# Macaron block on one core: first expert FFN on two hidden buffers, row 0's transposes inside the routing, another order of loads, stores and row ends

## What is computed

```
x = x + 0.5 * ffn(layernorm(x));  x = x + attn(layernorm(x));  x = x + 0.5 * ffn(layernorm(x))

ffn:  probs = softmax(x0 @ switch_w.T + switch_b)   # x0: all 512*512 values of a row, 8 experts
      gate, idx = top_k(probs, 2)
      h = gelu(xh @ w1[idx] + b1[idx])              # 16 heads of 32 features, the same expert for a whole row
      o = sum over k of gate[k] * (h @ w2[idx] + b2[idx])
      return (x + o) @ w3.T + b3
attn: q, k, v, a, g = split(x @ w_in.T); q = q*rsqrt(mean(q*q)); k = tanh(k); a = clip(sigmoid(a+2), 0.6, 0.9995)
      memory = linear recurrence of k*v with decay a along the tokens, in chunks of 64 tokens
      y = sigmoid(g)*(q*memory) + (1-sigmoid(g))*v;  return y @ w_out.T
```

## Time and profile before

| | before |
|---|---|
| runs, median (lowest to highest) | 574.57 us (573.95 to 575.01), 3 runs |
| the profiled execution | 573.66 us, of which 571.9 us are the span of the trace |
| PE busy | 507.7 us, 89% of the span |
| DVE / ACT / POOL busy | 417.1 / 232.1 / 137.1 us |
| mean granted clock of PE | 0.967 of full speed |
| chain of waits that ended last | PE 65%, DVE 16%, "issue" 7%, SP's queue 3%, POOL 3%, DMA 3%, ACT 2% |

### The profile page before, as it was taken

How to read it: one execution, slowest core, us unless ns; L and a number is a source line. 1 busy time by engine, 2 the same in 40 slices (tenths; PEclk the granted TensorE clock), 3 DMA queues, 4 the chain that set the end, 5 groups by cost and what they waited for, 6 DMA issues and landing times.

```text
span 571.9 us, 9061 instructions
## 1 busy us (share of the span) xinstructions
PE 507.7 (89%) x3372; PEld 361.8 (63%) x3372; DVE 417.1 (73%) x778; ACT 232.1 (41%) x390; POOL 137.1 (24%) x145
## 2 busy tenths in 40 slices
PE   0557899999899999989999999999998747999997
PEld 0444676567586666758666666866666634677776
DVE  4869887997864777796467788656868568988752
ACT  0145544432814233281422337243342237656540
POOL 5140004254002224401322430133330100321220
PEclk9976999999999999999999999999999877899999
DMA  8994004000002000010200000035535620013112
GB/s 345 409 388 202 1 1 166 1 0 1 37 19 92 2 0 2 1 38 19 92 0 0 0 0 37 18 128 194 188 144 182 216 74 2 19 47 119 41 53 92
DMA packets 15797, 48.21 MB, mean 84 GB/s; under 512 B 1169, under 2 KB 1169, under 8 KB 14225
## 3 DMA queue, kind: packets, MB, share of 16 engines
q1 hardware_dynamic: 15760, 47.73, 22.3%
HBM read 39.34 MB, written 8.39 MB: 83 GB/s over the span
## 4 chain that ended last, share of the span: by engine, by line
PE 65%; DVE 16%; issue 7%; SPq 3%; POOL 3%; DMA 3%; ACT 2%; DVEq 0%; POOLq 0%; ACTq 0%
PE bank L727 9%; PE bank L408 9%; PE bank L732 9%; PE bank L728 9%; PE bank L410 8%; PE bank L409 8%; DMA route_w<-in_switch_w 3%; SPq L434 2%; POOL rs L1132 2%; DVE h_lo L1342 2%; PE bank L531 2%; DVE xt_lo L1353 1%; PE bank L580 1%; PE bank L562 1%; PE bank L638 1%
## 5 line engine op out<-in xcount | busy, mean ns | idle before, releaser
L727 PE MATMUL bank<-xh,win_hi 128*128 128x512 f32 x300 | 133.7, 446 | 0.0
L728 PE MATMUL bank<-xl,win_hi 128*128 128x512 f32 x300 | 118.1, 394 | 0.0
L732 PE MATMUL bank<-xbf,win_lo 128*128 128x512 bf16 x312 | 85.3, 382 | 0.0
L1132 POOL TENSOR_TENSOR rs<-ms,neg_half 128x16 f32<-128x16 f32 x16 | 49.8, 3114 | 137.8 <-ACT ms L950 137.8
L727 PEld LDWEIGHTS bank<-xh,win_hi 128*128 128x128 f32 x300 | 56.4, 188 | 21.0 <-issue 3.2
L728 PEld LDWEIGHTS bank<-xl,win_hi 128*128 128x128 f32 x300 | 56.5, 188 | 11.1
L1119 POOL TENSOR_TENSOR xa<-xa,tables 128x512 f32<-128x512 f32 x28 | 38.9, 1401 | 71.4 <-DVE z_lo L1360 39.0
L408 PE MATMUL bank<-w_hi,z_hi 128*128 128x512 f32 x128 | 51.6, 403 | 0.0
L410 PE MATMUL bank<-w_hi,z_lo 128*128 128x512 f32 x128 | 50.1, 391 | 0.0
L409 PE MATMUL bank<-w_lo,z_hi 128*128 128x512 f32 x128 | 50.1, 391 | 0.0
L732 PEld LDWEIGHTS bank<-xbf,win_lo 128*128 128x128 bf16 x312 | 25.5, 98 | 35.5 <-issue 21.3
(11 more groups left out here) (199 smaller groups left out, 1010.4 us busy)
## 6 DMA issues: line engine op xcount, KB each, us to landing
raw<-in_w_in SPq DMA_DIRECT2D x4, 1280.0 KB, 9.9
route_w<-in_switch_w SPq DMA_DIRECT2D x4, 1280.0 KB, 5.4
route_w<-in_switch_w SPq DMA_DIRECT2D x9, 512.0 KB, 15.5
xa<-in_x SPq DMA_DIRECT2D x4, 1024.0 KB, 5.6
route_w<-in_switch_w SPq DMA_DIRECT2D x2, 2048.0 KB, 15.3
out<-x SPq DMA_DIRECT2D x16, 256.0 KB, 2.0
x_dram<-x1p SPq DMA_DIRECT2D x12, 256.0 KB, 2.0
xa<-x_dram SPq DMA_DIRECT2D x3, 1024.0 KB, 5.7
```

The costliest lines, as they stand in the source:

```text
L727: pe.matmul(bank[:], win_hi[:, c, r, k, :], xh[:, k, :], start=(k == 0), stop=False)
L728: pe.matmul(bank[:], win_hi[:, c, r, k, :], xl[:, k, :], start=False, stop=False)
L732: mm = pe.matmul(bank[:], win_lo[:, c, r, k, :], xbf[:, k, :], start=False, stop=(k == KC - 1))
L1132: pool.tensor_tensor(rs[:], ms[:], neg_half[:], ALU.pow).then_inc(s_rs, 1)
```

## The change

- **FFN 0** uses both hidden buffers, and ACT casts the second expert's half (`second_hi`); DVE splits chunk 1 right after chunk 0 and forms `w3_lo` after `split_hidden(0, 3)`.
- **Tables** are loaded in two parts: b3 ahead of the last routing weights, the rest behind them.
- **Attention chunk on ACT:** `y_out(b, c-1)` stands ahead of `decay`. The Gelu table is loaded after the first `t1_out` of the row end.
- **Row 3 on DVE:** the statistics of routing chunk 3 move from the gap of attention chunk 3 to behind chunk 2.
- **Routing:** row 0's transposes `t1(B, 0..3)` stand between routing chunks 1 and 2; `xt_split(B, 0..3)` ahead of `choose(1)`. ACT loads the Exp table before them.
- **Order on SP:** the load of `xa` between `late_weights` 2 and 3; after the routing first `xa1`, then, once it has landed, the stores of row 3, then `x1p`.
- **f = 5's normed tokens** are written by ACT (`row_norm(B + 1, 1, xnw)`, after the Gelu table, before `gelu(B, 0)`) and no longer by DVE.
- **POOL's bias adds** for f = 4 run as soon as the `xt_split`s are done.

```diff
 def hid_set(f, c):
-    return hid1 if is_late(f) and c % 2 else hid0
+    return hid1 if hid_bufs(f) == 2 and c % 2 else hid0      # hid_bufs: 2 if is_late(f) or f == 0
 # SP
-sp.dma_start(tables[:], tables_in).then_inc(s_small, 16)
+sp.dma_start(b3_half, tables_in[:, 0:D]).then_inc(s_b3l, 16)
 weight_load(NT - 1)
+sp.dma_start(tables[:, D:TABLES], tables_in[:, D:TABLES]).then_inc(s_small, 16)
...
 late_weights(2)
+sp.wait_ge(s_rna, 1)
+sp.dma_start(xa[:], row_of(x2_dram, 0)).then_inc(s_xa, 16)
 late_weights(3)
 sp.wait_ge(s_y, KC * B)
 late_piece(60, 64)
-sp.wait_ge(s_rna, 1)
-sp.dma_start(xa[:], row_of(x2_dram, 0)).then_inc(s_xa, 16)
+sp.wait_ge(s_rm, 2 * NT)
+sp.dma_start(xa1[:], row_of(x2_dram, 1)).then_inc(s_xa1, 16)
+sp.wait_ge(s_xa1, 16)
+for t in range(NT):
+    store_x2(B - 1, t, x1, job_last(f"A{t}"))
 sp.wait_ge(s_rna, 2)
 sp.dma_start(x1p[:], row_of(x2_dram, 2)).then_inc(s_xa2, 16)
-for t in range(NT):
-    store_x2(B - 1, t, x1, job_last(f"A{t}"))
-sp.wait_ge(s_rm, 2 * NT)
-sp.dma_start(xa1[:], row_of(x2_dram, 1)).then_inc(s_xa1, 16)
 # PE, route(phase)
+if phase == 1 and t == 2:
+    for c in range(KC):
+        t1(B, c, B - 1, False)
...
-for c in range(KC):
-    t1(B, c, B - 1, False)
-    if c == 1:
-        logits(1)
+logits(1)
 # ACT
 def ffn(f, begun):
     t1_out(f, 0)
+    load_table(ACT.Gelu)               # was the end of begun(), after t1_out(f, 1)
     t1_out(f, 1)
...
 # group(b, c), behind ms
+if c >= 1:
+    y_out(b, c - 1)
 act.activation(decay[:], src, ACT.Sigmoid, bias=two[:]).then_inc(s_ina, 1)
 src = bank(JOB_V)
-if c >= 1:
-    act.wait_ge(s_y, KC * b + c)
-    y_out(b, c - 1)
...
 # first_ffn: second_hi(0, c) behind every gelu(0, c)
 # end of attention
 route_norm(NT - 1)
-first_row()
+row_norm(B, 0, xn_0)
+load_table(ACT.Exp)
 for c in range(KC):
     t1_out(B, c)
 route_exp(1)
 load_table(ACT.Gelu)
+row_norm(B + 1, 1, xnw)                # waits for s_rm 2*NT and for xa1
 # POOL
+pool.wait_ge(s_xtl, KC * (B + 1))
+for c in range(KC):
+    residual_bias(B, c)                # was: each after z_split(B, c)
 # DVE, FFN 0
 split_hidden(0, 0, None)
-ve.wait_ge(s_w3h, 1)
-ve.scalar_tensor_tensor(out=w3_lo[:], ...).then_inc(s_w3l, 1)
+split_hidden(0, 1, None)
 for c in range(KC):
-    if c < KC - 1:
-        split_hidden(0, c + 1, job)
+    if c < 2:
+        split_hidden(0, c + 2, job_first(f"O{c}"))
+    if c == 1:
+        ve.wait_ge(s_w3h, 1)
+        ve.scalar_tensor_tensor(out=w3_lo[:], ...).then_inc(s_w3l, 1)
     z_split(0, c, x_bank[c])
 # DVE, attention(B - 1): gap of chunks 0 to 2: route_var(FEW + c, route_stats(FEW + c))
 # behind chunk 0, 1: route_norm(FEW + c); behind chunk 2: route_var(FEW + 3, route_stats(FEW + 3))
 route_norm(LAST + NT - 1)
+for c in range(KC):
+    xt_split(B, c)
 choose(1)
-xt_split(B, 0)
 select(0, B, 0)
-for c in range(1, KC):
-    xt_split(B, c)
 by_half(1)
 select(0, B, 1, lambda: gate(1))
 hidden_lo(B, 0)
 hidden_lo(B, 1)
-normalise(B + 1, 1)
```

More of the change, by code:

```diff
@@ L251, in ffn_input, with is_first, hid_bufs @@
             return xa, s_xa, 16 * f
+        def is_first(f):
+            return isinstance(f, int) and f == 0
+        def hid_bufs(f):
+            return 2 if is_late(f) or is_first(f) else 1
         def hid_set(f, c):
-            return hid1 if is_late(f) and c % 2 else hid0
+            return hid1 if hid_bufs(f) == 2 and c % 2 else hid0
         banks = [ctx.enter_context(nc.psum_tensor(f"bank{i}", [P, 512], F32)) for i in range(8)]
@@ L869, in gelu @@
                     act.wait_ge(s_h, H_JOBS * f + TOPK * c + k + 1)
-                    if is_late(f) or not (isinstance(f, int) and f == 0 and c == 0):
-                        bufs = 2 if is_late(f) else 1
-                        act.wait_ge(s_hl, H_JOBS * f + TOPK * (c - bufs) + k + 1)
+                    if not (is_first(f) and c < 2):
+                        act.wait_ge(s_hl, H_JOBS * f + TOPK * (c - hid_bufs(f)) + k + 1)
                     act.activation(hid_set(f, c)[0][:, k, :], h_bank[k][:], ACT.Gelu,
@@ L890, in second_hi @@
                     act.wait_ge(s_sel[1], f + 1)
-                else:
-                    act.wait_ge(s_ob, job_ffn(f, f"O{c - 1}") + 1)
+                elif c >= hid_bufs(f):
+                    act.wait_ge(s_ob, job_ffn(f, f"O{c - hid_bufs(f)}") + 1)
                 act.wait_ge(s_gelu, H_JOBS * f + TOPK * c + TOPK)
@@ L1036, in route_norm, with row_norm @@
                 ins.then_inc(s_rna, 1)
-            def first_row():
-                act.wait_ge(s_yl, KC * B)
-                act.wait_ge(s_xa, 16 * B)
+            def row_norm(f, row, dst):
+                src, *loaded = ffn_input(f)
+                if f == B:
+                    act.wait_ge(s_yl, KC * B)
+                else:
+                    act.wait_ge(s_rm, 2 * NT)
+                act.wait_ge(*loaded)
                 for t in range(NT):
-                    act.activation(xn_0[:, t * D:(t + 1) * D], xa[:, t, :], ACT.Identity,
-                                   scale=rstd[:, 0, t:t + 1], bias=shift[:, 0, t:t + 1]).then_inc(s_xn, 1)
+                    act.activation(dst[:, t * D:(t + 1) * D], src[:, t, :], ACT.Identity,
+                                   scale=rstd[:, row, t:t + 1], bias=shift[:, row, t:t + 1]).then_inc(s_xn, 1)
             attention(B - 1, lambda c: route_norm(c) if c == 2 else None)
@@ L1166, in _ @@
             pool.memset(set1[5][:].bitcast(F32), 0.0).then_inc(s_pad, 1)
-            for f in range(B, 2 * B):
+            pool.wait_ge(s_xtl, KC * (B + 1))
+            for c in range(KC):
+                residual_bias(B, c)
+            for f in range(B + 1, 2 * B):
                 for c in range(KC):
-                    if f == B:
-                        pool.wait_ge(s_obf, job_late(f, f"O{c}") + 1)
-                    elif c in (1, 2) and f + 1 < 2 * B:
+                    if c in (1, 2) and f + 1 < 2 * B:
                         pool.wait_ge(s_sel[c - 1], f + 2)
@@ L1337, in split_hidden @@
                         ve.wait_ge(s_ob, read_job + 1)
-                    if k == 1 and not (isinstance(f, int) and f == 0):
-                        ve.wait_ge(s_hh, KC * (f - 1) + c + 1)
+                    if k == 1:
+                        ve.wait_ge(s_hh, KC * f + c + 1)
                     else:
@@ L1533, in _, with within, behind @@
             own.base, own.n = base + (B - 2) * VE_ROW_STEPS, 0
-            attention(B - 1, lambda c: route_norm(FEW + c) if c < 2 else None,
-                      lambda c: route_var(FEW + c, route_stats(FEW + c)))
+            def within(c):
+                if c < NT - 1:
+                    route_var(FEW + c, route_stats(FEW + c))
+            def behind(c):
+                if c < 2:
+                    route_norm(FEW + c)
+                elif c == 2:
+                    route_var(FEW + NT - 1, route_stats(FEW + NT - 1))
+            attention(B - 1, behind, within)
             for t in range(NT):
```

14 lines of the change are left out of this document (8 added, 6 removed).

## The result

The changed kernel takes 563.96 us (562.88 to 564.23, 4 runs), the kernel before, timed beside it, 574.43 us: a ratio of 0.9815, with a 95% interval of 0.980 to 0.983. The forecast was 565.4, which is 1.4 us too high. The profiled execution of the changed kernel (563.94 us) has a span of 562.2 us where before had 571.9, so by the spans the gain is 9.7 us where the sum said 9.1. The other 0.8 us come from the step from a profiled execution to a median: the prediction added 0.9 us for it, and the changed kernel's profiled execution lies at its median.

What follows compares the result with a forecast made beforehand. PE was taken as the bound, busy 89% of the span. Gains 1.2 + 2.4 + 3.0 (row 3's attention and routing) + 2.8 - 0.3 = 9.1 us took 573.66 to 564.6; with 0.9 for the median, 565.5, stated as 565.4 (561.8 to 568.6).

Steps and rivals of the forecast that it cites:

- Start, 0: Kernel start: last routing weights come some 0.7 us earlier, but routing(0)'s last matmuls wait for code; taken as 0.
- FFN 0, -1.2: FFN 0: with two hidden buffers and `w3_lo` later, DVE reaches `win_lo` 1.2 us earlier; bounds 0.5 and 2.
- Row ends, -2.4: Ends of rows 0 to 2: earlier `y_out` removes PE's waits of 0.6, 0.9 and 0.9 us; bounds 0 and 3.3.
- Row 3's attention, -1.9: End of row 3's attention: moved statistics and earlier `y_out` remove PE's 1.45 us wait, plus 0.45; bounds 1.4 and 2.2.
- Routing(1), -1.1: Second routing: the 4.09 us code stop falls to 1.4, but transposes add 2.2 us and one more block border.
- Late FFN, -2.8: First late FFN: earlier splits, gelu 1.5 us earlier and less DVE work bring W0 of f = 4 2.8 us earlier.
- bias adds, +0.3: POOL's bias adds overlap `choose(1)` and delay its DVE operations by 0.3 us; bounds 0 and 2.
- item (c): Late FFN: DVE loses `normalise`, 1.91 us, and its later subtractions no longer meet a bias add (1.99 instead of 1.29).
- code is no limit: Rival for routing(1): all three PE stops were made by data; routing ends 3.5 us earlier, 561.9 us; chance 0.10.
- the row ends pay nothing: Rival for the row ends: POOL's `rs_wide` and bias adds stop DVE's early chain; 567.8 us; chance 0.13.
- `xa1`: Rival for the late FFN: this load is the new bound, landing 2 us later than alone; 567.4 us; chance 0.10.
- slower: Rival for the late FFN: ACT waits for the `xa1` load; at 17 us the kernel takes 575.8 us; chance 0.04.

Runs made afterwards that it cites:

- the eight equal kernels: The changed kernel and kernels 2, 3, 5, 6, 7, 9 and 10, equal up to row 1 (kernel 5 one instruction more); reach it between 175.04 and 176.49 us.
- kernel 4: Changed kernel with `w3_lo` between the first two splits, where DVE idles, instead of ahead of W0, two buffers kept; 562.68 us, ratio 0.9786.
- kernel 8: Kernel 4 and kernel 5 together; the empty instructions are left out by the compiler, so kernel 4 again but for one PE instruction; 563.60 us, ratio 0.9801.
- kernel 11: Changed kernel with the edits of kernel 4 and kernel 6 and 14 additional PE products in the late FFN; 560.00 us, ratio 0.9752.
- kernel 12: Kernel 11 with 9 further products between the first and second chunk's hidden products of the late FFN; 558.30 us, ratio 0.9722.
- kernel 1: Changed kernel with `y_out` back between `decay` and the copy of V; 566.95 us, ratio 0.9867.
- kernel 2: Changed kernel with SP's old order near row 3's end (`xa`, `x1p`, four stores, `xa1` behind the routing); 566.54 us, ratio 0.9861.
- kernel 6: Changed kernel with two of the four transposes in the routing and two behind the logits, their splits later on DVE; 561.64 us, ratio 0.9769.
- kernel 9: Changed kernel with 208 real semaphore instructions added to PE's program among row 3's input projection products; 563.08 us, ratio 0.9798.
- kernel 3: Changed kernel with row 0's transposes behind routing(1), the `xt_split`s where they were before, and no early Exp table load; 566.86 us, ratio 0.9869.
- kernel 7: Changed kernel with row B+1's normalisation back on DVE, behind the second chunk's subtractions, instead of on ACT; 563.63 us, ratio 0.9809.
- kernel 5: Changed kernel with 224 empty PE instructions ahead of the routing, which the compiler leaves out, so in effect a repetition; 564.07 us, ratio 0.9812.
- kernel 10: Changed kernel with 18 additional, unread PE products between the logits and the first hidden products; 563.02 us, ratio 0.9803.

## Why the prediction held, point by point

The mechanisms held, and the total is closer than its terms, which is partly luck: by the stages two terms were too large (FFN 0 by 0.6 us, routing(1) by 1.0) and three too small (the row ends by 0.8, row 3's attention by 0.3, the late FFN by 1.1).

**Start, 0.** The last 51 matmuls of routing(0) start at 36.31, not 36.17, with 0.95 us of "issue" ahead: the earlier weights bought nothing. That the wait for code is what took them was not tried; the experiments scatter from 36.17 to 36.62. The records speak for it: the one packet of the queue "instruction" between 30 and 39 us starts at 33.84, 2.5 us ahead of 36.31, and in routing(1) PE goes on 2.3 to 2.7 us behind the start of such a packet.

**FFN 0, -1.2.** Measured 0.6 to 0.8 us by `win_lo` and W0, which is inside the scatter of 1.5 us in that stage: the eight equal kernels reach `win_lo` between 62.36 and 63.83 us, the single trace of before at 63.53. So a gain from this edit as it was made is not shown. The step that was off is the walk of the chunks: I had chunk 2's low half at 55.7 and chunk 3's at 58.2, and got 56.4 and 58.8. The clock of PE, half until 53.1, was not in the walk. That `w3_lo` has no cover was right, and kernels 4, 8, 11 and 12 price it: some 1.6 us.

**Row ends, -2.4.** Mis-sized: 2.28 for rows 1 and 2 and 0.93 for row 0, 3.2 in all, just under the bound of 3.3 that I had named. I counted PE's wait at the first hidden products and no more. In the row end of row 1, PE waits 0.93, 0.38, 0.44 and 0.35 us before, 0.93, 0.34, 0.50 and 0.36 in kernel 1, and 0.35, 0.34 and 0.37 after: besides the first wait, the later one for `xt_lo` shrank from 0.50 to 0.34. In row 0 kernel 1 keeps 0.25 us of the gain: there PE's wait of 0.60 for ACT's gelu has become one of 0.34 for `h_lo`, which fits the earlier load of the Gelu table, though that was not tried alone.

**Row 3's attention, -1.9.** 2.20. By kernel 1 0.46 of it is the place of `y_out`.

**Routing(1), -1.1.** The mechanism was right in each part: the 4.09 us fell with the full DMA engines (kernel 2, 2.2 us), the borders lie where the count put them, and the end was pushed over one more (kernels 6 and 9). The size was off, 0.1 for 1.1. "Gets it 3.4 us later" is the step that was mis-sized: four blocks took 3.63 on average, 0.9 us more in all, and the last few matmuls behind them 0.4. So the reordered transfers gain 2.2 us in this stage and the transposes take 2.2 back (kernel 3).

**Late FFN, -2.8, and bias adds, +0.3.** 3.64 for 2.5. Gelu at T + 8.6 for T + 8.8, as walked. The adds ended at 454.67, 0.6 us ahead of `choose`, and met nothing. They are a near thing: at 2.2 us less of routing they meet `lmix` (kernel 9), and behind T they cost 3.1 us (kernel 3). My item (c) was wrong in part: DVE's loss of `normalise` is worth nothing (kernel 7). Its other half, the subtractions that no longer meet a bias add, is in the rows (1.29 and 1.28 us where before had 1.67 at 481.13 and 1.99 at 486.53) but was not tried alone. What my sum did not have is the granted clock: the third chunk's hidden products at half, and the second fall. Equal work differs by 0.9 us in this stage with it (the changed kernel and kernel 5), and kernels 10 and 12 gained 0.5 and 0.9 by keeping it up, each in one profiled execution. How the remaining 2.7 to 3.1 us divide was not separated: kernel 3 leaves 2.2 for the place of the splits, and the last part, from the second chunk's transposes of f = 5 (477.03, before 486.07) to W0, is 5.73 us where before had 6.44, of which the second fall is 0.2 to 0.3.

Of the rivals, "code is no limit" is refuted by kernels 2 and 9, "the row ends pay nothing" by kernel 1. `xa1` landed 5.7 us after its issue, undelayed. In the rival "slower" 575.8 us is the price of a load of 16 us, not of 17: by its own rule of a us for a us, 17 would give 576.8.

## What to carry to other kernels

Where PE's instructions are short (2.0 us for 256 of them here), its code is a transfer like any other: count instructions to the next border, keep the DMA engines empty there, and don't let the last few fall behind one. An idle stretch of PE costs twice if its clock falls with it, so price a stage at the clock that its rows grant, and repeat a run of equal code before a microsecond is put down to an edit. A long operation that moves should go where its engine idles, not merely behind the work that it delayed.

## What the runs showed of the hardware that I had not expected

- PE's code comes in blocks of 256 instructions, 16 KB (23 packets are 0.38 MB), so 64 bytes each: 208 real instructions ahead moved the stops by some 104 matmuls, took a 24th packet, and shortened the same work from 14.88 to 12.70 us. In nearly empty DMA the blocks were entered 3.3 to 4.2 us apart in the routing; beside full DMA the first came 5.9 us behind its start (kernel 2). Part of the variation is the packet itself (0.92 to 1.37 us in the changed kernel), part how soon it starts behind the entry into the block before it (1.1 to 1.3 us there, 1.8 once in kernel 5); why these vary is open.
- PE's clock fell to 1.2 GHz behind waits of 2.35 us (kernel 10), 1.89 (kernel 4) and 1.64 (kernel 12), and stayed at 2.4 GHz behind one of 1.91 us (the changed kernel): the length of the wait alone does not tell. 9 products that do nothing, in kernel 12, shortened the stage around them by 0.9 us in the one execution of each that was profiled.
- Small operations of DVE, a copy of 64x32 among them, took 1.2 to 1.4 us for 0.2 to 0.4 beside a bias add on POOL (kernel 3).
